# A DLRM tower on one core: products four samples wide in three banks, and a drain with moves on POOL

## The chip, the cores and the metric

One core of a Trainium2 chip runs the whole program. The metric is the device time of one execution in microseconds. The time before is the median of 3 runs.

## What is computed

The reference gathers 26 embedding rows of 64 numbers for each of 2048 samples and a dense vector of 256, and sends them through an interaction block and three layers:

```python
x = layer_norm(dense_t @ Wd.T, gd, bd)
y = layer_norm(jnp.einsum('bnd,ed->bne', sparse_t, Ws), gs, bs)
y = jnp.einsum('bne,pn->bep', y, Wsi)
y = layer_norm(y, gsi, bsi)
y = jnp.swapaxes(y, 1, 2)
T = jnp.concatenate([x[:, None, :], y], axis=1)
Z = jnp.einsum('bnd,bmd->bnm', T, T)
Zflat = Z[:, TRIL_I, TRIL_J]
out = layer_norm(Zflat @ Wl.T, gl, bl) * mask
h = jnp.concatenate([z, r_dense_t], axis=1)
h = jnp.maximum(h @ W_top1 + b_top1, 0.0)
h = jnp.maximum(h @ W_top2 + b_top2, 0.0)
y = h @ W_top3
```

All of it is fp32.

## The kernel before

The batch is cut into 16 units of 128 samples and each unit into four chunks of 32 samples. Each engine has its own program, and every one of them walks the same list of 75 steps. A step does a different stage for chunks of different age: a chunk is transposed (turn, L382) and its Gram products taken (gram, L391) one step after its number, mixed (mix, L405) and projected (project, L416) two steps after, and multiplied with itself (products, L430) four steps after. Work by unit follows: the products are moved to other partitions by DMA (MOVE_AT, 7), multiplied with the weights (flat, L442, in three pieces), normalised and turned back (turn_z, L450). Work by pairs of units (256 samples) is the top layers (top1, L465, in three pieces; top2, L526; top3, L533) and the dense branch (L544, L551, L556). Semaphores alone tie the engines together, and within one engine the order of the step's code holds.

POOL gathers the embedding rows, 26 indirect DMAs for a unit (L314), into three buffers. Before a chunk's gathers it waits until the chunk two before is transposed (turned).

The products of one chunk: tt holds, for WIDE samples at a time, their 34 columns (x, a one, 32 vectors) interleaved. One matmul takes all 32 vectors of WIDE samples as weights and all 34 columns of the same samples as the moving side. Its result holds every pair of the WIDE samples; only pairs of a sample with itself are used. With WIDE at 2 the result has 64 partitions, and two matmuls (q = 0, 1) fill one bank's 128 partitions. A chunk's eight groups of four samples are done in two rounds, one to bank_z and one to bank_t:

```python
WIDE = 2
TILE = PR * WIDE
ROUNDS = ((0, 4), (4, 8))
```

On ACT products_out (L675) copies each round's bank to zbig, with zc_ok counting NR copies a chunk. These banks are shared: bank_z lends its last 32 columns to scale_t (L976), bank_t takes the transposes of turn, bank_u takes the results of mix. squares (L662) come behind products_out on ACT, xcol (L688) and place_sum_x (L697) behind those.

After the last chunk's turn, the drain begins (steps beyond TAIL = 63). There the last two units' flat, turn_z and gains_z have places of their own, tables at flat_of, turn_z_of and gains_z_of. The moves of the last unit are shared out: SP issues those of sample classes j = 0, 1, and ACT, in move_rest (L774), those of j = 2, 3, six of each. relu1 (L736) rectifies the first layer's two pairs of column blocks, gains_z (L727) scales the rows of a turned unit, z_rows (L682) copies the moved products. open_last (L475) starts the last half batch's first layer from the dense part, last1 (L490) finishes it.

Of the kernel before, what the change touches and what calls it, by code (L numbers as in the profile page):

```python
# [44 lines left out]
NU = B // UNIT  # L45
# [16 lines left out]
GROUPS = ((0, 4), (4, 7), (7, 10), (10, 13))  # L62
PIECES = ((0, 2), (2, 4), (4, 6))
HALVES = ((0, 2), (2, 4)), ((4, 6), (6, 7)), ((7, 9), (9, 10)), ((10, 12), (12, 13))
WIDE = 2
TILE = PR * WIDE
ROUNDS = ((0, 4), (4, 8))
NR = len(ROUNDS)


# [93 lines left out]

def gains_z_of(s):
    if s > TAIL + 2:
        return {TAIL + 6: NU - 2, TAIL + 8: NU - 1}.get(s)
    return unit(s, GAINZ_AT)


def half_of(s, steps):
    return steps.index(s) if s in steps else None


def dlrm(nc, x_in, out):
    with ExitStack() as ctx:
# [6 lines left out]
        def sem(name):  # L183
            return ctx.enter_context(nc.semaphore(name))
# [81 lines left out]
        y_ok, sq_ok, ssum_ok, sstd_ok, srs_ok, t_ok = (  # L266
            sem("y_ok"), sem("sq_ok"), sem("ssum_ok"), sem("sstd_ok"), sem("srs_ok"), sem("t_ok"))
        xcol_ok, z_done, zc_ok, sumcol_ok = sem("xcol_ok"), sem("z_done"), sem("zc_ok"), sem("sumcol_ok")
        zs_in, zr_ok = [sem("zs_in0"), sem("zs_in1")], sem("zr_ok")
        flat_done, hst_ok, hmv_ok, hstd_ok, hrs_ok, zn_ok = (  # L270
            sem("flat_done"), sem("hst_ok"), sem("hmv_ok"), sem("hstd_ok"), sem("hrs_ok"), sem("zn_ok"))
        znt_done, zt_ok = sem("znt_done"), sem("zt_ok")
# [27 lines left out]
        @block.gpsimd  # L300
        def _(pool):
            pool.wait_ge(ids_ok, 1)
            for u in range(NU):
                e = u % EB
                for c in range(4):
                    after(pool, mixed, 4 * (u - EB) + min(c + 2, 4))
                    after(pool, turned, 4 * u + c - 1)
                    for part, (t0, t1) in enumerate(HALVES[c]):
                        if part == 1:
                            after(pool, z_done, NR * (4 * u + c - 5) + 1)  # L310
                        for t in range(t0, t1):
                            for a in range(2):
                                col = 2 * TILES * u + 2 * t + a
                                pool.indirect_dma_start(  # L314
                                    emb[:, e, t, D * a:D * a + D], None, x_in["tables"],
                                    bass.IndirectOffsetOnAxis(ap=ids[:, col:col + 1], axis=0),
                                ).then_inc(emb_in[e][c], 16)

        @block.sync
        def _(sp):  # L320
# [47 lines left out]
        def _(pe):  # L368
# [26 lines left out]
            def mix(u, h):  # L395
                e = u % EB
                pieces = mix_pieces(h)
                if u == 0 and h == 0:
                    pe.wait_ge(pre_v, 9)
                pe.wait_ge(scaled, 4 * u + h + 1)  # L400
                after(pe, u_ok, 4 * u + h)
                for c, (t, lo, cnt) in enumerate(pieces):
                    o = PR * (lo - GRP * h)
                    w0 = PR * (lo - first_sample(t))
                    mm = pe.matmul(  # L405
                        bank_u[:, o:o + PR * cnt], emb[:, e, t, :],
                        mix_w[:, t, :, :].rearrange("p s v -> p (s v)")[:, w0:w0 + PR * cnt],
                        start=(c == 0), stop=(c == len(pieces) - 1), skip_group_check=True)
                mm.then_inc(mixed, 1)
# [9 lines left out]
            def products(u, h, i):  # L419
# [1 line left out]
                    pe.wait_ge(t_ok, 4 * u + h + 1)  # L421
                    pe.wait_ge(xcol_ok, u + 1)
                after(pe, zc_ok, NR * (4 * u + h))
                o_bank = (bank_z, bank_t)[i]
                g0, g1 = ROUNDS[i]
                for g in range(g0, g1):
                    for q in range(4 // WIDE):
# [146 lines left out]
            for s in range(STEPS):  # L574
# [11 lines left out]
                    project(*c)  # L586
                pd = chunk(s, PROD_AT)
                if pd:
                    products(*pd, 0)
                    products(*pd, 1)  # L590
                for piece in range(3):
                    j = top1_of(s, piece)
                    if j is not None:
# [5 lines left out]
                j = top2_of(s)  # L599
                if j is not None:  # L600
                    top2(j)
                if s == TAIL + 6:
                    open_last()
                i = x_of(s, 0)
                if i is not None:
                    dense_x(i)
# [9 lines left out]
                j = top3_of(s)  # L616
                if j is not None:
                    top3(j)
                a = half_of(s, LAST1_AT)
                if a is not None:  # L620
                    last1(a)
# [9 lines left out]
        def _(act):  # L631
# [38 lines left out]
            def products_out(u, h, i):  # L670
                act.wait_ge(z_done, NR * (4 * u + h) + i + 1)
                if h == 0 and i == 0:
                    after(act, zs_in[u % 2], 12 * 16 * (u // 2))
                g0, g1 = ROUNDS[i]
                act.copy(zbig[:, u % 2, :, C0:CZ, 8 * h + g0:8 * h + g1],  # L675
                         (bank_z, bank_t)[i][:, 0:ZC * WIDE * (g1 - g0)].rearrange("p (g c w) -> p w c g", c=ZC, w=WIDE)
                         ).then_inc(zc_ok, 1)

            def z_rows(u):
                act.wait_ge(zs_in[u % 2], 12 * 16 * (u // 2 + 1))  # L680
                after(act, flat_done, u)
                act.copy(zr[:, :, :].rearrange("p s (j g) -> p s j g", j=4),  # L682
                         zs[:, :, :, :].rearrange("p j s g -> p s j g")).then_inc(zr_ok, 1)
# [81 lines left out]
                act.wait_ge(y_out, LAST + 1)  # L765
                act.dma_start(out[:, SUP * LAST:SUP * LAST + SUP], yrow[:, :]).then_inc(stored, 16)

            def move_rest():
                act.wait_ge(zc_ok, 4 * NR * NU)
                act.wait_ge(sumcol_ok, NU)  # L770
                act.wait_ge(zr_ok, NU - 1)
                for j in range(2, 4):
                    for part in range(3):
                        act.dma_start(rows_to(j, part), rows_from((NU - 1) % 2, j, part)  # L774
                                      ).then_inc(zs_in[(NU - 1) % 2], 16)

            def relu2(j):
                act.wait_ge(top2_done, j + 1)
                after(act, top3_done, j)
# [12 lines left out]
            for s in range(STEPS):  # L792
# [48 lines left out]
                if se:  # L841
                    root_e(*se)
                if pd:
                    products_out(*pd, 0)
                    products_out(*pd, 1)
                if pj:
                    squares(*pj, 0)
                    squares(*pj, 1)
                if pd == (NU - 1, 3):
                    move_rest()  # L850
                u = col_of(s, XCOL_AT)
                if u is not None:
                    xcol(u)
# [291 lines left out]
```

## Time and profile before

| | |
|---|---|
| median of 3 runs | 590.68 us (590.22 to 592.27) |
| profiled execution | 590.11 us |
| its span, first to last instruction | 588.3 us |
| mean granted TensorE clock | 0.983 of full |
| busy: PE, DVE, ACT, POOL | 523.2, 431.7, 339.3, 394.8 us |

The profile gives busy time by engine and the chain of work that ended last, the groups of instructions by line with what ended the idle time before them, and the timeline. PE is the matmul side of TensorE and PEld its weight loads. An fp32 matmul leaves two records, a transpose one. Times in a timeline are from the start of the span; the "us" of a row reaches to the modelled end of its last instruction, so rows of pipelined matmuls overlap by some tenths of a microsecond, and the distance from one row's start to the next one's start is the time that the work takes.

### The profile page before, as it was taken

Reading aid. Unit: us, or ns where it says so; the run is one execution under the profiler, and the core shown is the slowest. Engines: PE = TensorE matmul, PEld = TensorE weight load, DVE = VectorE, ACT = ScalarE, POOL = GpSimd, SP = SyncE. Lnnn points to the kernel's source line nnn. Section 1 sums busy time; section 2 is a strip of 40 time slices with the busy share of each in tenths; the row PEclk is TensorE's granted clock in tenths of the full one; section 3 lists DMA queues with packets and bytes.
Section 4 is the critical chain, followed back from the end, with each engine's and each line's share of the span. In section 5 each row is a group of like instructions: output and inputs, shape, how many; then the busy total and the mean of one; then the engine's idle time right before and its main releaser. Section 6 shows DMA issues by size and latency. Waiting matters only on the chain.

```text
span 588.3 us, 11685 instructions
## 1 busy us (share of the span) xinstructions
PE 523.2 (89%) x4327; PEld 382.3 (65%) x4327; DVE 431.7 (73%) x806; ACT 339.3 (58%) x731; POOL 394.8 (67%) x420
## 2 busy tenths in 40 slices
PE   0557889597999999997999999998999999989888
PEld 0435656474778667776677767766777767856657
DVE  3579998689677977697877967796787977787210
ACT  1235666466657765575766765675657765766223
POOL 5777777777777777777777777777777777750000
PEclk9997999899899999999999999999999999999999
DMA  6911121212111121212121221212121211110100
GB/s 214 372 47 26 28 54 27 53 28 52 29 42 38 39 62 28 52 30 71 28 46 33 45 56 35 45 31 69 29 52 27 52 31 43 38 34 17 27 0 1
DMA packets 28152, 29.89 MB, mean 51 GB/s; under 512 B 9784, under 2 KB 20544, under 8 KB 27712
## 3 DMA queue, kind: packets, MB, share of 16 engines
q0 software_dynamic: 13312, 13.66, 12.2%
q1 hardware_dynamic: 14456, 15.29, 8.2%
q8 instruction: 35, 0.57, 0.4%
q10 hardware_dynamic: 328, 0.20, 0.1%
q14 instruction: 21, 0.17, 0.1%
HBM read 23.01 MB, written 0.01 MB: 39 GB/s over the span
## 4 chain that ended last, share of the span: by engine, by line
POOL 46%; PE 26%; issue 19%; DMA 4%; DVE 3%; ACT 1%; ACTq 1%; POOLq 0%; SPq 0%
POOL emb L314 46%; PE bank_h L442 5%; PE bank_u L405 4%; DMA emb<-in_tables,ids 3%; PE bank_m L465 3%; PE bank_y L416 3%; PE bank_g L391 2%; PE bank_z L430 2%; PE bank_t L382 2%; PE bank_t L430 1%; PE bank_m L526 1%; DVE part L910 1%; ACTq L774 1%; PE bank_g L490 1%; PE bank_m L533 0%
## 5 line engine op out<-in xcount | busy, mean ns | idle before, releaser
L314 POOL DMA_INDIRECT emb<-in_tables,ids x416 | 394.6, 949 | 130.3 <-issue 123.1
L662 ACT ACTIVATE sq<-tt 128x512 f32<-128x512 f32 x128 | 131.1, 1133 | 4.6 <-DVE tt L963 3.4
L932 DVE TENSOR_TENSOR prod<-bank_g,emb 128x512 f32<-128x512 f32 (+1 forms) x64 | 37.6, 588 | 89.0 <-PE bank_g L391 88.5
L442 PE MATMUL bank_h<-wz,zr 128*128 128x512 f32 x192 | 93.2, 610 | 3.1 <-ACT zt L727 2.1
L405 PE MATMUL bank_u<-mix_w,emb 128*128 128x192 f32 (+4 forms) x512 | 86.0, 314 | 9.7 <-DVE emb L951 9.7
L405 PEld LDWEIGHTS bank_u<-mix_w,emb 128*128 128x128 f32 x512 | 80.3, 200 | 10.9 <-DVE emb L951 10.9
L963 DVE TENSOR_TENSOR tt<-bank_y,biasc 128x512 f32<-128x512 f32 x128 | 81.9, 681 | 2.5 <-PE bank_y L416 2.5
L644 ACT COPY embt<-bank_t 128x512 f32<-128x512 f32 (+1 forms) x64 | 32.5, 507 | 82.4 <-PE bank_t L382 82.2
L980 DVE TENSOR_TENSOR tt<-tt,bank_z 128x1024 f32<-128x1024 f32 x64 | 78.1, 1220 | 2.2
L970 DVE TENSOR_REDUCE ssum<-sq 128x32 f32<-128x1024 f32 x64 | 77.5, 1211 | 1.1 <-ACT sq L662 1.0
L416 PE MATMUL bank_y<-us,proj 64*128 64x512 f32 x256 | 73.0, 647 | 0.7 <-ACT us L654 0.7
L430 PEld LDWEIGHTS bank_z<-tt 128*64 128x64 f32 x1024 | 35.4, 137 | 48.5 <-issue 47.4
L391 PE MATMUL bank_g<-gram_w,embt 128*128 128x128 f32 x416 | 61.9, 290 | 1.7 <-ACT embt L644 1.7
L382 PE MATMUL bank_t<-eye,emb 128*128 128x128 f32 x208 | 36.3, 290 | 27.5 <-DMA emb<-in_tables,ids 27.5
L654 ACT COPY us<-bank_u 128x512 f32<-128x512 f32 x64 | 37.5, 586 | 40.2 <-PE bank_u L405 40.1
L391 PEld LDWEIGHTS bank_g<-gram_w,embt 128*128 128x128 f32 x416 | 55.2, 202 | 2.7 <-ACT embt L644 2.5
L382 PEld LDWEIGHTS bank_t<-eye,emb 128*128 128x128 f32 x208 | 25.1, 146 | 48.5 <-DMA emb<-in_tables,ids 37.5
L442 PEld LDWEIGHTS bank_h<-wz,zr 128*128 128x128 f32 x192 | 33.8, 190 | 30.7 <-issue 26.8
L649 ACT ACTIVATE std<-var 128x8 f32<-128x8 f32 (+1 forms) x64 | 13.6, 212 | 56.4 <-DVE var L942 54.1
L430 PE MATMUL bank_z<-tt 128*64 128x68 f32 x1024 | 44.5, 229 | 0.0
L430 PE MATMUL bank_t<-tt 128*64 128x68 f32 x1024 | 41.2, 223 | 0.0
L465 PE MATMUL bank_m<-zt,w 128*128 128x256 f32 x168 | 40.8, 379 | 0.0
(121 smaller groups left out, 622.5 us busy)
## 6 DMA issues: line engine op xcount, KB each, us to landing
emb<-in_tables,ids POOLq DMA_INDIRECT x416, 2.4
zs<-zbig SPq DMA_DIRECT2D x62, 40.5 KB
zs<-zbig SPq DMA_DIRECT2D x62, 36.0 KB
dense<-in_dense SPq DMA_DIRECT2D x8, 256.0 KB, 5.1
wfull<-in_wfull SPq DMA_DIRECT2D x1, 2048.0 KB, 10.2
wz<-in_wrows SPq DMA_DIRECT2D x1, 1536.0 KB, 13.2
w<-in_w SPq DMA_DIRECT2D x1, 1280.0 KB, 13.9
zs<-zbig SPq DMA_DIRECT2D x62, 16.5 KB
```

What stands on the lines that cost most here:

```text
L314: pool.indirect_dma_start(emb[:, e, t, D * a:D * a + D], None, x_in["tables"], bass.IndirectOffsetOnAxis(ap=ids[:, col:col + 1], axis=0),) ...
L382: mm = pe.transpose(bank_t[:, P * (t - t0):P * (t - t0) + P], emb[:, e, t, :], eye[:, :])
L391: mm = pe.matmul(bank_g[:, o:o + P], embt[:, k % 2, o:o + P], gram_w[:, :], start=True, stop=True)
L405: mm = pe.matmul(bank_u[:, o:o + PR * cnt], emb[:, e, t, :], mix_w[:, t, :, :].rearrange("p s v -> p (s v)")[:, w0:w0 + PR * cnt], start=( ...
L416: mm = pe.matmul(bank_y[a][:, :], proj[q, :], us[q, h % 2, :], start=True, stop=True)
L430: mm = pe.matmul(o_bank[TILE * q:TILE * q + TILE, o:o + ZC * WIDE], some[:, C0 * WIDE:ZC * WIDE], some, start=True, stop=True)
L442: mm = pe.matmul(bank_h[:, :], zr[:, s, :], wz[:, s, :], start=(s == 0), stop=(s == SLOTS - 1))
L465: mm = pe.matmul(bank_m[:, SUP * (c % 2):SUP * (c % 2) + SUP], w1[:, t, P * c:P * c + P], rhs, start=(t == 3), stop=(t == 2))
L662: A(sq[:, GRP * a:GRP * a + GRP, :].rearrange("p (q w) v -> p q v w", w=WIDE), tt[:, u % 2, q0:q0 + n, C0:ZC, :], ACT.Square).then_inc(sq_ ...
L963: TT(tt[:, u % 2, q0:q0 + n, C0:ZC, :], bank_y[a][:, :].rearrange("p (q w v) -> p q v w", w=WIDE, v=PR), biasc[:, :].unsqueeze(1).unsqueez ...
L970: dve.tensor_reduce(ssum[:, h % 2, :], sq[:, :, :], AX.X, ALU.add).then_inc(ssum_ok, 1)
L980: TT(y, y, srs.rearrange("p (q w) -> p q w", w=WIDE).unsqueeze(2).broadcast_to([P, n, PR, WIDE]), ALU.mult).then_inc(t_ok, 1)
```

## The change

WIDE becomes 4: one matmul takes four samples, 128 weight columns and 136 moving columns, and fills all 128 partitions (so the loop over q has one turn). Three such results fit in a bank, so the eight groups go in three rounds of 3, 3 and 2, to bank_z, bank_t and bank_u. Mix, which writes bank_u, gets a wait for the copies of the chunk products that used it. tt, zbig and rows_from follow WIDE. In the drain the six moves of move_rest go from ACT's queue to POOL's, behind its last gather, with a semaphore of their own (zs_rest); gains_z of unit 14 moves from step TAIL + 6 to TAIL + 5, where it stands between the two rectified pairs; open_last moves from behind top2 in step TAIL + 6 to behind top3 in step TAIL + 7.

```diff
-WIDE = 2
+WIDE = 4
 TILE = PR * WIDE
-ROUNDS = ((0, 4), (4, 8))
+ROUNDS = ((0, 3), (3, 6), (6, 8))
...
     if s > TAIL + 2:
-        return {TAIL + 6: NU - 2, TAIL + 8: NU - 1}.get(s)
+        return {TAIL + 5: NU - 2, TAIL + 8: NU - 1}.get(s)
...
+            pool.wait_ge(zc_ok, 4 * NR * NU)
+            pool.wait_ge(sumcol_ok, NU)
+            pool.wait_ge(zr_ok, NU - 1)
+            for j in range(2, 4):
+                for part in range(3):
+                    pool.dma_start(rows_to(j, part), rows_from((NU - 1) % 2, j, part)
+                                  ).then_inc(zs_rest, 16)
...
                 after(pe, u_ok, 4 * u + h)
+                after(pe, zc_ok, NR * (4 * u + h - 2))
...
-                o_bank = (bank_z, bank_t)[i]
+                o_bank = (bank_z, bank_t, bank_u)[i]
...
-                    products(*pd, 0)
-                    products(*pd, 1)
+                    for i in range(NR):
+                        products(*pd, i)
...
-                if s == TAIL + 6:
-                    open_last()
                 i = x_of(s, 0)
...
                     top3(j)
+                if s == TAIL + 7:
+                    open_last()
...
             def z_rows(u):
-                act.wait_ge(zs_in[u % 2], 12 * 16 * (u // 2 + 1))
+                if u < NU - 1:
+                    act.wait_ge(zs_in[u % 2], 12 * 16 * (u // 2 + 1))
+                else:
+                    act.wait_ge(zs_in[u % 2], 12 * 16 * (u // 2) + 6 * 16)
+                    act.wait_ge(zs_rest, 6 * 16)
...
-                    products_out(*pd, 0)
-                    products_out(*pd, 1)
+                    for i in range(NR):
+                        products_out(*pd, i)
...
-                if pd == (NU - 1, 3):
-                    move_rest()
```

On the PE, in a step of the steady part, from gram to the next step's transposes. Before:

```order
L391 MATMUL bank_g<-gram_w,embt 128x128 x3
L416 MATMUL bank_y<-us,proj 128x512 x2
L430 MATMUL bank_z<-tt 64x68 x8
L430 MATMUL bank_t<-tt 64x68 x8
L442 MATMUL bank_h<-wz,zr 128x512 x2
```

After (the lines are numbered anew, L438 is products):

```order
L398 MATMUL bank_g<-gram_w,embt 128x128 x3
L424 MATMUL bank_y<-us,proj 128x512 x2
L438 MATMUL bank_z<-tt 128x136 x3
L438 MATMUL bank_t<-tt 128x136 x3
L438 MATMUL bank_u<-tt 128x136 x2
L450 MATMUL bank_h<-wz,zr 128x512 x2
```

Sixteen matmuls with 64 result partitions and 68 columns have become eight with 128 and 136.

On ACT, in the drain, from the last unit's products to the scaling of unit 14 (L736 rectifies, L727 scales, L682 is z_rows). Before:

```order
L675 COPY zbig<-bank_t 128x2x34x4
L774 DMA zs<-zbig 22x1x192
L774 DMA zs<-zbig 48x1x192
L774 DMA zs<-zbig 54x1x192
L774 DMA zs<-zbig 22x1x192
L774 DMA zs<-zbig 48x1x192
L774 DMA zs<-zbig 54x1x192
L736 ACTIVATE h<-bank_m,vecs 128x256 x2
L682 COPY zr<-zs 128x768
L736 ACTIVATE h<-bank_m,vecs 128x256 x2
L727 ACTIVATE zt<-bank_h,vecs 128x128 x3
```

After:

```order
L683 COPY zbig<-bank_t 128x4x34x3
L683 COPY zbig<-bank_u 128x4x34x2
L748 ACTIVATE h<-bank_m,vecs 128x256 x2
L739 ACTIVATE zt<-bank_h,vecs 128x128 x3
L694 COPY zr<-zs 128x768
L748 ACTIVATE h<-bank_m,vecs 128x256 x2
L784 ACTIVATE h<-bank_m,vecs 128x256 x2
```

The six moves are gone from ACT's queue, the scaling stands ahead of z_rows and the second pair, and z_rows waits for POOL's moves too.

On the PE, at the end of the drain, from flat of unit 15 on. Before:

```order
L442 MATMUL bank_h<-wz,zr 128x512 x6
L526 MATMUL bank_m<-h,w 128x256 x8
L475 MATMUL bank_t<-dense,w 128x128 x2
L475 MATMUL bank_u<-dense,w 128x128 x2
L475 MATMUL bank_y<-dense,w 128x128 x4
L450 MATMUL bank_h<-eye,zn 128x128 x3
L533 MATMUL bank_m<-h,vecs 1x256 x2
L490 MATMUL bank_g<-dense,w 128x128 x2
```

After:

```order
L450 MATMUL bank_h<-wz,zr 128x512 x6
L534 MATMUL bank_m<-h,w 128x256 x8
L458 MATMUL bank_h<-eye,zn 128x128 x3
L541 MATMUL bank_m<-h,vecs 1x256 x2
L483 MATMUL bank_t<-dense,w 128x128 x2
L483 MATMUL bank_u<-dense,w 128x128 x2
L483 MATMUL bank_y<-dense,w 128x128 x4
L498 MATMUL bank_g<-dense,w 128x128 x2
```

The eight matmuls of open_last have gone from before turn_z to behind top3.

## Rows read from the trace of the kernel before

**Rows 1.** The page: busy times by engine, and the chain by line.

```profile
PE 523.2 (89%) x4327; PEld 382.3 (65%) x4327; DVE 431.7 (73%) x806; ACT 339.3 (58%) x731; POOL 394.8 (67%) x420
...
POOL emb L314 46%; PE bank_h L442 5%; PE bank_u L405 4%; DMA emb<-in_tables,ids 3%; PE bank_m L465 3%; PE bank_y L416 3%; PE bank_g L391 2%; PE bank_z L430 2%; PE bank_t L382 2%; PE bank_t L430 1%; PE bank_m L526 1%; DVE part L910 1%; ACTq L774 1%; PE bank_g L490 1%; PE bank_m L533 0%
```

**Rows 2.** Groups: busy us, mean ns | idle before; waits: us in total, times, longest.

```profile
L314 POOL DMA_INDIRECT emb<-in_tables,ids x416 | 394.6, 949 | 130.3 <-issue 123.1 <-DVE ids L871 3.9 <-PE bank_t L382 3.0
...
POOL emb L314 <- issue: 123.1, 404, 0.3
```

**Rows 3.** Stretches of 65 us from 170 to 495 us, their sum and mean.

```profile
sum 325.00, PE 315.13 PEld 230.85 DVE 258.06 ACT 209.61 POOL 245.76; mean PE 63.03 PEld 46.17 DVE 51.61 ACT 41.92 POOL 49.15
```

**Rows 4.** Waits of PE, 148 to 528 and 60 to 148 us; timeline at 147.

```profile
PE bank_t L382 <- DMA emb<-in_tables,ids: 11.6, 10, 2.5
...
PE bank_t L382 <- DMA emb<-in_tables,ids: 12.2, 5, 4.9
...
147.36 1.07 PE L382 MATMUL bank_t<-eye,emb 128*128 128x128 f32 x4 [4.16 <-DMA emb<-in_tables,ids]
```

**Rows 5.** Timeline of PE in one step: start us, us, what.

```profile
304.92 1.13 PE L416 MATMUL bank_y<-us,proj 64*128 64x512 f32 x4
305.98 0.69 PE L430 MATMUL bank_z<-tt 128*64 128x68 f32 x16
306.50 0.64 PE L430 MATMUL bank_t<-tt 128*64 128x68 f32 x16
307.07 1.13 PE L465 MATMUL bank_m<-dense,w 128*128 128x256 f32 x4
```

**Rows 6.** Groups by form: the gram matmuls.

```profile
L391 PE MATMUL bank_g<-gram_w,embt 128*128 128x128 f32 x416 | 61.9, 290 | 1.7 <-ACT embt L644 1.7
```

**Rows 7.** The chain in the drain: start us, us, what.

```profile
524.42 2.49 DMA emb<-in_tables,ids
...
561.78 5.39 PE bank_h L442 x12
...
574.15 4.66 PE bank_g L490 x40
```

**Rows 8.** Timeline of ACT in a short step.

```profile
196.00 0.33 ACT L688 COPY tt<-xs 128x128 f32<-128x128 f32 x1
196.22 0.47 ACT L644 COPY embt<-bank_t 128x384 f32<-128x384 f32 x1
```

**Rows 9.** Groups by form on ACT.

```profile
L662 ACT ACTIVATE sq<-tt 128x512 f32<-128x512 f32 x128 | 131.1, 1133 | 4.6 <-DVE tt L963 3.4
...
L675 ACT COPY zbig<-bank_z 128x272 f32<-128x272 f32 x64 | 24.7, 386 | 5.2 <-PE bank_z L430 3.1 <-ACT yrow L788 0.3
L644 ACT COPY embt<-bank_t 128x384 f32<-128x384 f32 x48 | 23.1, 481 | 35.2 <-PE bank_t L382 35.0
```

**Rows 10.** Timeline of ACT in the drain (ACTq issues the moves).

```profile
549.00 5.14 ACTq L774 DMA_DIRECT2D zs<-zbig  x6
554.24 0.84 ACT L736 ACTIVATE h<-bank_m,vecs 128x256 f32<-128x256 f32 x2 [5.27 <-issue]
555.73 0.83 ACT L682 COPY zr<-zs 128x768 f32<-128x768 f32 x1 [0.65 <-DMA zs<-zbig]
559.75 0.84 ACT L736 ACTIVATE h<-bank_m,vecs 128x256 f32<-128x256 f32 x2 [3.19 <-PE bank_m L465]
```

**Rows 11.** Timeline of PE in the drain.

```profile
552.57 0.49 PE L450 MATMUL bank_h<-eye,zn 128*128 128x128 f32 x3
555.13 1.13 PE L465 MATMUL bank_m<-dense,w 128*128 128x256 f32 x4 [2.07 <-ACT h L736]
...
570.46 0.61 PE L475 MATMUL bank_t<-dense,w 128*128 128x128 f32 x4
...
571.35 1.06 PE L475 MATMUL bank_y<-dense,w 128*128 128x128 f32 x8
572.65 0.55 PE L450 MATMUL bank_h<-eye,zn 128*128 128x128 f32 x3 [0.24 <-DVE zn L1014]
```

More of the change, by code:

```diff
@@ L268, in dlrm @@
         xcol_ok, z_done, zc_ok, sumcol_ok = sem("xcol_ok"), sem("z_done"), sem("zc_ok"), sem("sumcol_ok")
-        zs_in, zr_ok = [sem("zs_in0"), sem("zs_in1")], sem("zr_ok")
+        zs_in, zs_rest, zr_ok = [sem("zs_in0"), sem("zs_in1")], sem("zs_rest"), sem("zr_ok")
         flat_done, hst_ok, hmv_ok, hstd_ok, hrs_ok, zn_ok = (
@@ L675, in products_out @@
                 act.copy(zbig[:, u % 2, :, C0:CZ, 8 * h + g0:8 * h + g1],
-                         (bank_z, bank_t)[i][:, 0:ZC * WIDE * (g1 - g0)].rearrange("p (g c w) -> p w c g", c=ZC, w=WIDE)
+                         (bank_z, bank_t, bank_u)[i][:, 0:ZC * WIDE * (g1 - g0)].rearrange("p (g c w) -> p w c g", c=ZC, w=WIDE)
                          ).then_inc(zc_ok, 1)
             def z_rows(u):
-                act.wait_ge(zs_in[u % 2], 12 * 16 * (u // 2 + 1))
+                if u < NU - 1:
[3 more added lines that the diff above has]
+                    act.wait_ge(zs_rest, 6 * 16)
                 after(act, flat_done, u)
@@ L766, in last_store @@
                 act.dma_start(out[:, SUP * LAST:SUP * LAST + SUP], yrow[:, :]).then_inc(stored, 16)
[L768 to L775, printed above, removed]
             def relu2(j):
```

## The prediction, made before the run

> **What bounds the kernel now.** I read the page's busy times and its chain first, then the groups of POOL, then the stretches, then the waits of the PE, and last the timeline of one step. The page shows the PE busy 89% of the span and a chain in which the gathers of line L314 hold 46% [rows 1]. POOL issues 416 gathers of 949 ns and sits 0.30 us before each (123.1 us over 404) [rows 2], so a unit of 26 gathers takes 26 x 1.25 = 32.5 us, and the 16 units fill 519 us. That is the pace. The PE is close behind it: over five stretches of 65 us (two units each) it is busy 315.1 us of 325 at a granted clock of 1.00, the 2.4 GHz level [rows 3]. From 148 to 528 us its only idle time is ten waits for gathered rows, 11.6 us together; from 60 to 148 us there are 12.2 us more [rows 4]. So the PE has 11.6 us to give away over the last 47 steps, 0.25 us a step. Anything above that, per step, becomes the new pace.
>
> **Part 1, products four samples wide.** In a step the two rounds of products stand between project (L416, at 304.92) and the next work: they start at 305.98, and the next line starts at 307.07 [rows 5]. That is 1.09 us for 32 records (each fp32 matmul leaves two records: 16 matmuls, and x16 in each of two rows), 34 ns a record of 68 columns. One column at full array width costs 5.39 us / (12 x 512) = 0.877 ns for wide records, and 4.66 / (40 x 128) = 0.91 ns for narrow ones, both back to back in the drain [rows 7]. At 0.877 a record of 68 columns would take 60 ns. The 34 ns can only be two records running side by side, one in each half of the array's columns (q = 0 and q = 1 write partitions 0 to 63 and 64 to 127).
>
> The change has 8 matmuls of 128x136 in a step, 16 records, and each fills the array, so nothing runs beside it: 16 x 136 x 0.877 = 1.91 us. The step grows by 1.91 - 1.09 = 0.82 us. The useful work is the same; the wide form computes 4x4 blocks of sample pairs, of which 4 of 16 are kept, where the narrow one kept 2 of 4. Ends of this price: if the wide record ran like project's, which pays (305.98 - 304.92) / (4 x 512) = 0.52 ns a column [rows 5], the block would take 1.13 us and the step would grow by 0.04; if it ran at the mean of the gram matmuls, 149 ns for 128 columns (61.9 us over 416 records) [rows 6], it would take 2.53 us and the growth would be 1.44. The first needs half an array; the second mean has waits for the ACT in it. I take 0.82 and hold 0.7 to 1.0 as likely.
>
> Of the 1.09 us now, 16 pairs x 60 ns explain 0.95, so 0.14 us at most is the cost of entering and leaving the half-width form. If it is paid after the change too, the growth is 0.96, and the result 47 x 0.14 = 6.6 us later. The Trainium skill (TensorEngine Tiling, section Key Properties) says that a change of tiling mode, not of tile alone, drains the engine. By that rule one mode fewer in each step saves this time, which is the 0.82; no run here shows it apart.
>
> From the wait that ends at 147 us to the last transpose (chunk 63, at 527) there are 47 steps. The wait before them, 4.16 us [rows 4], is longer than the 4 x 0.82 us gained since the last one, so the lag starts near zero there; earlier steps cost nothing because they lie in the 12.2 us of waits. The lag at chunk 63 is 47 x 0.82 - 11.6 = **26.9 us**. POOL is then held by the PE (it waits for turned), but it has two PE steps, some 17 us, for at most 8 x 1.25 + 2.49 = 12.5 us of gathers and landing [rows 2, 7], so no new wait comes from it. With no gather waits left, all of the PE's time is work.
>
> **Part 2, three banks and three copies.** The ACT copies now take 272 elements in 386 ns; from 384 in 481 ns [rows 9] the slope is 0.85 ns. 408, 408 and 272 elements make 500 + 500 + 386 = 1.39 us against 0.77: 0.62 us more a step. The third bank's copy can start only after the products' end, so by my estimate it ends near P + 2.5 us (P = start of products; 1.91, some 0.2 to start, 0.39), against P + 1.6 now (1.09 in place of 1.91). Squares (1133 ns each, overlapping a little) and in some steps one more copy (0.33 us) follow, and only then the next embt copy: in one short step it starts at 196.22, the moment its predecessor in the queue is through [rows 8]. The PE comes to it 0.8 us later than now and the ACT 0.9 us later, so about nothing is lost in most steps, and a few tenths in the two short steps of every eight: 12 x 0.17, call it **2 us**. Unknown is how runs of three elements are written instead of four. Lower end: no cost. Upper end: the rate of the scattered writes of the squares, 1133 ns for 512 [rows 9], 2.2 ns each. Three copies then take 2.4 us. That is a rival below. The new wait before mix (bank_u free) asks for what the transposes before it have waited for already; it costs 0. The DVE waits for the same copies before it scales with bank_z; its queue is busy 51.6 us of 65 in two units [rows 3], so 0.
>
> **Part 3, the drain.** Three blocks of products (chunks 60 to 62) put 2.5 us before the last one, and its own copies end 0.9 us later in the block and a little more: the moves start some 3.1 us later than 549.00 (relative to the lag). Now ACT issues six moves in 5.14 us, and the first rectified pair sits behind them until 554.24 [rows 10], though its products were done before the PE's turn_z at 552.57 [rows 11]. After the change POOL issues them, so the pair runs at 552.6 + 3.3 = 555.9, 1.7 us later than now. The PE's third piece starts 0.9 us after the pair and takes 4.6 us (555.13 to 559.75 now [rows 10, 11]), so it ends at 555.9 + 0.9 + 4.6 = 561.4. The row scaling of unit 14 (1.16 us) goes in beside it. The moved rows: six on POOL from 552.1. Lower bound for one is ACT's 0.84 us with 1.6 us to landing (554.14 to 555.73), upper is a gather's 1.25 us with its 2.49 [rows 2, 7]: landing at 558.7 to 562.1, copied 0.83 us later, 559.5 to 562.9. I take the middle, under the PE's 561.4. So flat of unit 15 starts between 561.4 and 562.9, against 561.78 now [rows 7]: **0**, up to +1.1. Nothing else is queued behind POOL's wait: it has no gathers left.
>
> open_last goes the other way. Now its 16 records (570.46 to 572.4) fill the gap in which the DVE normalises, and turn_z waits only 0.24 us more [rows 11]. After the change they stand behind turn_z and top3; the gap stays (relu2 and the root are still before the normalising), and 16 x 0.117 = **1.9 us** come onto the path.
>
> **Sum.** 26.9 + 2 + 0 + 1.9 = 30.8 us. The profiled execution took 590.11 us (588.3 of span and 1.8 around it): 590.1 + 30.8 = **620.9 us**. That execution lies 0.6 us under the median of the runs, 590.68, so 621 is about 30.5 us over the median, 5.1%.
>
> **The rivals.**
> - The copies become the loop (0.12). If runs of three and two are written at the squares' rate, the last copy ends near P + 3.5, the squares near P + 5.6, and the next embt copy and the gram behind it come 0.9 us late in two short steps of eight. In favour: the squares' 1133 ns. Against: runs of four cost nothing over contiguous writes [rows 9]. 12 x 0.9 us = 11 more in place of my 2, with a little in other steps: 632 us.
> - The wide products are nearly free (0.07), the case that ends on the other side. It decides at 0.25 us a step, that is 1.34 us for the block or 84 ns a record. Only project's half-array rate (70 ns) is under that. Steady state stays at POOL's 32.5 us; in the drain the pair starts 1.5 us earlier, flat 1.7 to 3.6 us earlier, open_last takes back 1.9: 588.4 to 590.3, say 589.4 us. Against it: 117 ns back to back for full-width records of 128 columns [rows 7].
> - A fixed cost in every matmul, now paid half as often (0.05). If 25 ns of each of the 34 ns were fixed and not shared, the 16 records saved would give back 0.4 us: growth 0.42, lag 47 x 0.42 - 11.6 = 8.1, with 2 + 1.9: 602 us. Against it: 128 and 512 columns cost nearly the same per column [rows 7]. The Trainium skill (TensorEngine Tiling, section Instruction Overhead) gives such a fixed cost of about 60 cycles a matmul; the trace, with 34 ns a record for 68 columns, leaves no room for it.
> - Something I have not seen, such as DVE and ACT waiting in turn (0.06): 635 us and more.
>
> **How the numbers follow.** My forecast has 0.70. Its own range: growth 0.7 to 1.0 gives lags of 21.3 to 35.4, the rest 1 to 6: 612 to 631. With the copies' case the range is 607 to 635, which leaves out under 2 in 10. About 0.3% is what a measurement of this kernel can tell from no change. Faster needs the nearly free case and a quick POOL: 0.03; within 0.3% is the rest of it: 0.04; slower: 0.93.
>
> **What would show it.** Right: POOL waits for bank_t transposes in nearly every chunk; the PE's gather waits vanish after 150 us; product blocks of about 1.9 us, 117 to 125 ns from record to record; units of 34.8 us or a little over; the six POOL moves done by 559 plus the lag; 1.9 us of open_last behind top3. Wrong: units still at 32.5 us (the block is under 1.34 us), or embt and us copies that the PE waits for in most steps (the ACT's loop), or POOL moves of well over 1.25 us each.

## The result and the profile after

The changed kernel takes 615.45 us (median of 4 runs, 615.4 to 615.79), against 591.42 us for the kernel before in the same session: a ratio of 1.042 (95% interval 1.0403 to 1.044), so slower. (The ratios of this document are not quotients of the two medians beside them; here the medians give 1.0406.) The profiled execution took 615.44 us with a span of 613.3 us, 25.0 us more than the 588.3 before. The forecast was 621.0, with a range of 607 to 635.

The page of the changed kernel, busy times and the chain by engine and by line:

```profile
PE 567.7 (93%) x3303; PEld 433.7 (71%) x3303; DVE 439.5 (72%) x806; ACT 371.3 (61%) x779; POOL 398.0 (65%) x426
...
PE 81%; POOL 8%; DVE 4%; issue 3%; DMA 2%; ACT 2%; SPq 0%; ACTq 0%; POOLq 0%
PE bank_h L450 13%; PE bank_m L473 10%; PE bank_u L413 10%; PE bank_y L424 9%; PE bank_z L438 8%; POOL emb L314 8%; PE bank_g L398 7%; PE bank_t L438 6%; PE bank_u L438 4%; PE bank_m L534 4%; PE bank_t L389 4%; DMA emb<-in_tables,ids 2%; PE bank_m L541 1%; PE bank_m L552 1%; DVE part L911 1%
```

The gathers held 46% of the chain [rows 1] and hold 8% now. The PE is busy 44.5 us more with 1024 records fewer. Its waits (us in total, times, longest) from 148 to 555 us, and below them those of POOL over the span:

```profile
PE bank_t L389 <- DMA emb<-in_tables,ids: 2.2, 1, 2.2
...
POOL emb L314 <- issue: 119.4, 391, 0.6
POOL emb L314 <- PE bank_t L389: 22.3, 19, 2.0
```

The one wait of the PE for rows is at 147.82 and stands against the 4.16 us before [rows 4]; the ten after it are gone, and now POOL waits for the PE, 19 times. That is once or twice a unit; the forecast had it in nearly every chunk. Five stretches of 70 us, a little over two units each, from 170 to 520 us, their sum and mean:

```profile
sum 350.00, PE 349.95 PEld 268.85 DVE 267.35 ACT 233.63 POOL 253.52; mean PE 69.99 PEld 53.77 DVE 53.47 ACT 46.73 POOL 50.70
```

The PE has 0.05 us left in 350, where it had 9.9 in 325 [rows 3]. Four chunks, from one unit's first transposes to the next one's, now take 34.2 us (183.59 to 525.94 is ten units), where 34.8 was forecast; before, the same ten took 32.4 each (181.56 to 505.62, in both kernels chunks 20 to 60). The PE's timeline of one step, which answers to [rows 5]:

```profile
303.71 1.13 PE L424 MATMUL bank_y<-us,proj 64*128 64x512 f32 x4
304.77 0.96 PE L438 MATMUL bank_z<-tt 128*128 128x136 f32 x6
305.57 0.86 PE L438 MATMUL bank_t<-tt 128*128 128x136 f32 x6
306.27 0.63 PE L438 MATMUL bank_u<-tt 128*128 128x136 f32 x4
306.73 1.03 PE L473 MATMUL bank_m<-dense,w 128*128 128x256 f32 x4
307.59 1.46 PE L473 MATMUL bank_m<-zt,w 128*128 128x256 f32 x6
```

The block of products takes 306.73 - 304.77 = 1.96 us, 122 ns a record, in place of 1.09 us. But the first four records behind it take 307.59 - 306.73 = 0.86 us, and took 308.04 - 307.07 [rows 5] = 0.97 us; the row that followed before:

```profile
308.04 1.46 PE L465 MATMUL bank_m<-zt,w 128*128 128x256 f32 x6
```

The step is therefore longer by 0.76 us. The turns of the two kernels, compared chunk by chunk, fall apart by 0.75 to 0.77 us in most steps in which the kernel before had no wait, and by about 0.70 in the step behind a long one.

The copies of ACT by form (busy us, mean ns | idle before them), for [rows 9]:

```profile
L683 ACT COPY zbig<-bank_t 128x408 f32<-128x408 f32 x64 | 41.0, 640 | 9.0 <-PE bank_t L438 8.9
L683 ACT COPY zbig<-bank_z 128x408 f32<-128x408 f32 x64 | 32.2, 504 | 15.1 <-PE bank_z L438 14.5 <-ACT yrow L791 0.3
L683 ACT COPY zbig<-bank_u 128x272 f32<-128x272 f32 x64 | 26.0, 407 | 0.0
```

The PE in the drain, which answers to [rows 7, 11], and POOL's and ACT's part of it, which answer to [rows 10]:

```profile
569.42 0.86 PE L438 MATMUL bank_z<-tt 128*128 128x136 f32 x6
...
576.68 1.13 PE L473 MATMUL bank_m<-dense,w 128*128 128x256 f32 x4 [0.60 <-ACT h L748]
...
579.80 1.46 PE L473 MATMUL bank_m<-zt,w 128*128 128x256 f32 x6
583.29 7.11 PE L450 MATMUL bank_h<-wz,zr 128*128 128x512 f32 x12 [2.02 <-ACT zr L694]
590.24 3.62 PE L534 MATMUL bank_m<-h,w 128*128 128x256 f32 x16
595.88 0.55 PE L458 MATMUL bank_h<-eye,zn 128*128 128x128 f32 x3 [2.02 <-DVE zn L1015]
596.36 1.02 PE L541 MATMUL bank_m<-h,vecs 128*1 128x256 f32 x4
597.31 0.71 PE L483 MATMUL bank_t<-dense,w 128*128 128x128 f32 x4
597.86 0.61 PE L483 MATMUL bank_u<-dense,w 128*128 128x128 f32 x4
598.30 1.06 PE L483 MATMUL bank_y<-dense,w 128*128 128x128 f32 x8
599.20 0.61 PE L498 MATMUL bank_g<-dense,w 128*128 128x128 f32 x4
```

```profile
572.32 3.39 POOL L323 DMA_DIRECT2D zs<-zbig  x6 [30.34 <-ACT zbig L683]
```

```profile
575.79 0.84 ACT L748 ACTIVATE h<-bank_m,vecs 128x256 f32<-128x256 f32 x2 [3.76 <-PE bank_m L473]
581.36 1.16 ACT L739 ACTIVATE zt<-bank_h,vecs 128x128 f32<-128x128 f32 x3 [4.74 <-PE bank_m L473]
582.40 0.83 ACT L694 COPY zr<-zs 128x768 f32<-128x768 f32 x1
```

The scaling of unit 14 stands behind the third piece, z_rows behind the scaling, and flat waits 2.02 us for both. Where the 25.0 us come from:

| place | lag over before, us | since the line above |
|---|---|---|
| turn of chunk 63 (526.96, now 547.20) | 20.2 | |
| flat of unit 15 (561.78, now 583.29) | 21.5 | +1.3 |
| top2 (567.01, now 590.24) | 23.2 | +1.7 |
| turn_z (572.65, now 595.88) | 23.2 | 0 |
| last1 | 25.1 | +1.9 |
| end of span | 25.0 | -0.1 |

Three groups of runs follow. The last group, and of the second group the run with one change of half, were on two other chips, on which the kernel before takes 763.65 and 773.73 us (medians of 35 and 29). The executions read there are interrupted by pauses, of 2 to 3 us in the place read most closely (the narrow kernel with its moves on POOL, 400 to 406 us: POOL idle 2.19 us, DVE 2.93, ACT 3.26, the PE going on in pieces). Of these runs only the ratios and undisturbed stretches of the timeline are read. The ratios compare, of each kernel, only its executions within 1.5% of its fastest, and the medians are of all, so the two can point different ways.

### The profile page after: what moved, and what is told of

It reads as the page before. It is cut to its first block, busy times and chain, and to the rows that moved or that the text cites. A ratio compares the mean times of both kernels' runs of the same rounds, so it can differ in the third digit from the quotient of the medians.

```text
span 613.3 us, 9685 instructions
## 1 busy us (share of the span) xinstructions
PE 567.7 (93%) x3303; PEld 433.7 (71%) x3303; DVE 439.5 (72%) x806; ACT 371.3 (61%) x779; POOL 398.0 (65%) x426
## 3 DMA queue, kind: packets, MB, share of 16 engines
q0 software_dynamic: 13504, 13.85, 11.6%
## 4 chain that ended last, share of the span: by engine, by line
PE 81%; POOL 8%; DVE 4%; issue 3%; DMA 2%; ACT 2%; SPq 0%; ACTq 0%; POOLq 0%
PE bank_h L450 13%; PE bank_m L473 10%; PE bank_u L413 10%; PE bank_y L424 9%; PE bank_z L438 8%; POOL emb L314 8%; PE bank_g L398 7%; PE bank_t L438 6%; PE bank_u L438 4%; PE bank_m L534 4%; PE bank_t L389 4%; DMA emb<-in_tables,ids 2%; PE bank_m L541 1%; PE bank_m L552 1%; DVE part L911 1%
## 5 line engine op out<-in xcount | busy, mean ns | idle before, releaser
L450 PE MATMUL bank_h<-wz,zr 128*128 128x512 f32 x192 | 91.5, 603 | 2.0 <-ACT zr L694 2.0
L413 PE MATMUL bank_u<-mix_w,emb 128*128 128x192 f32 (+4 forms) x512 | 84.0, 309 | 9.0 <-DVE emb L952 9.0
L413 PEld LDWEIGHTS bank_u<-mix_w,emb 128*128 128x128 f32 x512 | 78.5, 196 | 9.7 <-DVE emb L952 9.7
L438 PEld LDWEIGHTS bank_z<-tt 128*128 128x128 f32 x384 | 48.8, 190 | 48.2 <-issue 47.3
L438 PE MATMUL bank_z<-tt 128*128 128x136 f32 x384 | 61.5, 297 | 0.0
L438 PE MATMUL bank_t<-tt 128*128 128x136 f32 x384 | 55.0, 279 | 0.0
L438 PEld LDWEIGHTS bank_t<-tt 128*128 128x128 f32 x384 | 49.3, 190 | 0.0
L683 ACT COPY zbig<-bank_t 128x408 f32<-128x408 f32 x64 | 41.0, 640 | 9.0 <-PE bank_t L438 8.9
```

The costliest lines, as they stand in the source:

```text
L413: mm = pe.matmul(bank_u[:, o:o + PR * cnt], emb[:, e, t, :], mix_w[:, t, :, :].rearrange("p s v -> p (s v)")[:, w0:w0 + PR * cnt], start=( ...
L438: mm = pe.matmul(o_bank[TILE * q:TILE * q + TILE, o:o + ZC * WIDE], some[:, C0 * WIDE:ZC * WIDE], some, start=True, stop=True)
L450: mm = pe.matmul(bank_h[:, :], zr[:, s, :], wz[:, s, :], start=(s == 0), stop=(s == SLOTS - 1))
```

## The experiments

**Theory.** The steady part costs some 20 us since wide products lose the overlap of two half-width matmuls; the drain's edits cost the rest. **Rivals.** The copies or the third round cost it, not the products; or the drain's edits do.

### The wide products alone, and the drain alone

The first is the changed kernel with move_rest on ACT, gains_z and open_last as before. The second is the kernel before with the three drain edits of the change:

```diff
-        return {TAIL + 6: NU - 2, TAIL + 8: NU - 1}.get(s)
+        return {TAIL + 5: NU - 2, TAIL + 8: NU - 1}.get(s)
...
-                if s == TAIL + 6:
-                    open_last()
+                if s == TAIL + 7:
+                    open_last()
...
-                    move_rest()
```

(move_rest goes to POOL as in the change.)

> The wide products in three banks alone, with the drain as it was before (moves on ACT, scaling of unit 14 in step TAIL + 6, open_last behind top2). Theory: the whole loss of the steady part is the PE's block of products, so the last transposes stand at 547.2 us as in the changed kernel (20.2 us late) and POOL waits for bank_t. In the drain: last copies end at 572.0, ACT issues until 577.2, the first pair at 577.3, third piece to 582.8, second pair, scaling, flat of unit 15 at about 584.9 (changed kernel: 583.3), but open_last lies in its gap again, 1.9 us back, and if flat runs at the full clock as before, 1.7 us more: 613.2 us in all, 2 us under the changed kernel. Rival: the drain edits bring what they were put in for, so without them it takes 617 us or more.

> The three drain edits alone, with products two samples wide. Theory: the PE's steady part is that of the kernel before, last transposes at 527.0. The first pair runs at 552.8 in place of 554.2, the third piece ends at 558.2, but the scaling of unit 14 waits for that piece (it overwrites rows that the piece reads), so the scaling takes 558.3 to 559.5, the copy of the moved rows until 560.3, flat of unit 15 starts at 560.3 (1.5 us earlier), open_last costs 1.9: 590.5 us; if flat falls to the low clock as in the changed kernel, 592.2. Rival (my prediction's picture): the scaling runs beside the third piece and flat starts at 558.2 to 559: 588.5 us.

Measured, with the kernel before at 590.37 us (median of 19): wide alone 612.92 us (612.74 to 613.07), ratio 1.037 (1.0343 to 1.0398); the drain alone 592.27 us (590.87 to 593.92, 10 runs), ratio 1.002 (1.0004 to 1.0036). So the products carry 22.5 of the changed kernel's surplus of some 25 us, and the other 2.5 come with the drain's edits (0.4 of them ahead of the drain, where the two kernels do the same work: the last products start at 568.98 and 569.42). The PE of the wide kernel in its drain:

```profile
568.98 0.86 PE L431 MATMUL bank_z<-tt 128*128 128x136 f32 x6
...
584.41 5.39 PE L443 MATMUL bank_h<-wz,zr 128*128 128x512 f32 x12 [2.07 <-ACT zt L728]
```

From the last products to flat it takes 15.43 us, the changed kernel 583.29 - 569.42 = 13.87: the drain's edits do bring flat 1.6 us forward. They lose it again, and 2 us more, in two places, open_last (1.9 us) and flat itself (5.39 became 7.11). The second place is told by the drain alone, PE timeline:

```profile
560.46 7.11 PE L449 MATMUL bank_h<-wz,zr 128*128 128x512 f32 x12 [2.03 <-ACT zr L693]
...
574.49 1.11 PE L482 MATMUL bank_t<-dense,w 128*128 128x128 f32 x4
```

and by the stretches of 2 us in it, first the drain alone, then the changed kernel (us, busy us of the engines, granted clock, DMA share, GB/s):

```profile
562.00:564.00 2.00, 2.00 (x4) 0.86 (x3) 0.00 (x0) 0.00 (x0) 0.00 (x0) 0.50 0.00 0
...
576.00:578.00 2.00, 2.00 (x12) 2.00 (x11) 0.00 (x0) 0.00 (x0) 0.00 (x0) 0.50 0.00 0
```

```profile
584.00:586.00 2.00, 2.00 (x3) 0.69 (x3) 0.00 (x0) 0.00 (x0) 0.00 (x0) 0.53 0.00 0
586.00:588.00 2.00, 2.00 (x4) 0.87 (x3) 0.00 (x0) 0.00 (x0) 0.00 (x0) 0.62 0.00 0
```

Behind the gap ahead of flat the clock was granted at the lower of its two levels, 1.2 GHz, for about 3.4 us (worked out from the shares above, 0.53 and 0.62 of full), and flat pays for it. The drain alone met it twice, in flat and again in open_last, which took 574.49 to 577.95, 3.46 us for 1.89. Its profiled span is 3.8 us over that of before and its median only 1.9 us, so not every execution has both.

### What in the products costs: rounds, copies, or overlap

The narrow kernel, first with three rounds, banks, copies and the wait before mix, as the change has them:

```diff
-ROUNDS = ((0, 4), (4, 8))
+ROUNDS = ((0, 3), (3, 6), (6, 8))
...
+                after(pe, zc_ok, NR * (4 * u + h - 2))
...
-                o_bank = (bank_z, bank_t)[i]
+                o_bank = (bank_z, bank_t, bank_u)[i]
```

> Products two samples wide, but in three rounds (3, 3, 2 groups) to three banks with three copies, and the new wait of mix: what the change does to ACT and the banks, without the wide matmuls. Theory: the PE's block stays 1.1 us and the copies cost about 0.2 us more a step on ACT, which has room: 590 to 592 us. Rival (copies and the bank wait form a loop with the PE): 595 us or more, with waits of PE for zbig or embt copies.

Measured 590.64 us (590.0 to 592.43, 10 runs), ratio 1.0004 (0.9988 to 1.002). The page's waits of the PE:

```profile
PE bank_t L382 <- DMA emb<-in_tables,ids: 27.7, 19, 5.0
```

That is the total of the span, and before it was 27.5 us in 18 waits, of which [rows 4] has the two parts that matter here. So the third round, the third copy and the wait before mix cost nothing. The copies here have half the elements (204, 204 and 136, in 329, 401 and 290 ns), so the length of the wide ones isn't covered by this run, and is read from the changed kernel: no wait of the PE for ACT in its steady part.

Then the narrow kernel with the loop over q outside that over g, so that all matmuls of one half of the columns come before those of the other, in each round. The work is the same:

```diff
-                for g in range(g0, g1):
-                    for q in range(4 // WIDE):
+                for q in range(4 // WIDE):
+                    for g in range(g0, g1):
```

> The kernel before with only the order of its narrow products changed: in each round all four groups of the lower half (q = 0), then all four of the upper half (q = 1), instead of lower and upper by turns. Same matmuls, same number, same data. Theory: 34 ns a record came from two halves running side by side; in turn they take about 60 ns, the block 1.8 to 1.9 us in place of 1.09, and the kernel becomes as slow as the wide one, 609 to 614 us. Rival (a fixed cost in every matmul, or weight loads, set the 34 ns): nothing changes, 590 to 592 us.

Measured 599.09 us (596.06 to 599.54), ratio 1.0118 (1.008 to 1.0156): slower, by 8.7 us where 19 to 24 were expected. Neither had said this. Its PE timeline tells why (start us, us):

```profile
301.24 0.80 PE L430 MATMUL bank_z<-tt 128*64 128x68 f32 x13
301.83 0.27 PE L430 MATMUL bank_t<-tt 128*64 128x68 f32 x1
301.88 0.22 PE L430 MATMUL bank_z<-tt 128*64 128x68 f32 x1
301.94 0.22 PE L430 MATMUL bank_t<-tt 128*64 128x68 f32 x1
...
302.06 0.75 PE L430 MATMUL bank_t<-tt 128*64 128x68 f32 x13
302.74 1.13 PE L465 MATMUL bank_m<-dense,w 128*128 128x256 f32 x4
```

Records of bank_z and bank_t alternate in time although the code has all of bank_z first: the upper half of bank_z runs beside the lower half of bank_t. The block takes 1.50 us. The same timeline accounts for the time of the whole:

```profile
533.35 0.49 PE L382 MATMUL bank_t<-eye,emb 128*128 128x128 f32 x3
...
569.49 7.08 PE L442 MATMUL bank_h<-wz,zr 128*128 128x512 f32 x12 [2.07 <-ACT zt L727]
```

The transposes of chunk 63 are 533.35 - 526.96 = 6.4 us late, the three blocks behind them add 1.2, and flat took 7.08 in place of 5.39: 9.3 us of the 9.4 between the two spans (597.7 and 588.3). The block has three changes of half, and several matmuls overlap at each. So I made one with a single change, by ordering lower bank_z, lower bank_t, upper bank_z, upper bank_t:

```diff
-                for g in range(g0, g1):
-                    for q in range(4 // WIDE):
+                halves = ((0, 0), (0, 1), (1, 0)) if i == 0 else ((1, 1),)
+                for q, r in halves:
+                    o_bank = (bank_z, bank_t)[r]
+                    g0, g1 = ROUNDS[r]
+                    for g in range(g0, g1):
```

> As halves in turn, but the lower halves of both banks first and then the upper halves of both, so that there is one place in a step where lower gives way to upper, in place of three. In the trace of the run with three such places the block took 1.50 us, 0.41 under the 1.91 that 32 x 60 ns make, 0.14 for each place where the two halves overlap. Theory: with one place the block takes about 1.77 us, the step grows by 0.68, and 47 steps less the 15.5 us of slack that the two traces show make 16.5 us more at the last transposes: 606 to 611 us. Rival (something else in the reordering cost the 9 us): as slow as halves in turn, 599 us.

This one ran on the third chip: 784.61 us (781.75 to 788.65), ratio 1.0202 (1.012 to 1.0285). Its time on a chip like the first can't be read from that. Its block can:

```profile
302.99 0.69 PE L431 MATMUL bank_z<-tt 128*64 128x68 f32 x8
303.51 0.46 PE L431 MATMUL bank_t<-tt 128*64 128x68 f32 x5
...
303.99 0.46 PE L431 MATMUL bank_z<-tt 128*64 128x68 f32 x5
304.28 0.64 PE L431 MATMUL bank_t<-tt 128*64 128x68 f32 x8
304.85 0.48 PE L466 MATMUL bank_m<-dense,w 128*128 128x256 f32 x1
```

1.86 us for the same 32 records, 58 ns each, in place of 34; 1.77 was expected. (The five records from 303.99 to 304.28, which nothing overlaps, also take 58 ns each.) The same 16 matmuls take 1.86 us with one change of half, 1.50 with three and 1.09 where every matmul changes it; the wide form takes 1.96. That shows what the 0.82 us of the forecast rested on: the narrow form's advantage is the running side by side of its two halves.

### The drain

On the second chip, the changed kernel with open_last back where it was (behind top2), and the kernel before with the moves on POOL and nothing else. The edit of the first:

```diff
+                if s == TAIL + 6:
+                    open_last()
...
-                if s == TAIL + 7:
-                    open_last()
```

> The changed kernel with open_last back behind top2 (step TAIL + 6); all else as changed. Theory: open_last's 16 records fill the 2 us in which the DVE normalises the last unit, so 1.9 us come back: 613.6 us. Rival: the gap is filled by something else or the matmuls then delay turn_z: within 0.3 us of the changed kernel, 615.4.

> The kernel before with only the six last moves issued by POOL. Theory: the first pair starts when its products are done, 552.8 in place of 554.2, so the third piece, second pair and scaling, and with them flat of unit 15, come 1.4 us earlier, at 560.3: 588.7 us against 590.1 of the kernel before. Rival: POOL's moves land so late (after 560) that z_rows takes over as the end: no change.

Then both with the scaling of unit 14 freed of the third piece. The last half batch gets its own buffer for turned rows, so nothing that the piece reads is overwritten, and the scaling runs between the rectified pairs. In the narrow one (the wide one has the same edit; both have open_last behind top2):

```diff
-        return {TAIL + 6: NU - 2, TAIL + 8: NU - 1}.get(s)
+        return {TAIL + 5: NU - 2, TAIL + 8: NU - 1}.get(s)
...
+        zt_last = sb("zt_last", [P, 3, SUP])
...
-                if u % 2 == 0:
+                to = zt if u < NU - 2 else zt_last
+                if u % 2 == 0 and u < NU - 2:
```

> The kernel before with the moves on POOL and the scaling of unit 14 between the two pairs, and with a buffer of its own for the last two units' scaled rows, so that this scaling need not wait for the third piece of top1; open_last stays behind top2. Theory: scaling runs at 553.7 to 554.8 beside the third piece, the moved rows are copied by 556.5, and flat of unit 15 starts right behind the third piece at 558.2, 3.6 us earlier than before: 586.5 us. Rival: the copies of moved rows or stats come late and take the place of the scaling: 588 us or more.

> The changed kernel with that buffer and with open_last back. Theory: relative to the changed kernel, flat starts at 581.3 in place of 583.3 with no idle time of 2 us before it, so it also keeps the high clock (5.3 us in place of 7.0), and open_last gives back 1.9: 2.0 + 1.7 + 1.9 = 5.6 us, 609.8 us. If the low clock in flat does not hang on that idle time: 611.5 us.

These three were repeated on the third chip, for the ratios:

> The same kernel as e5, on another chip. Theory: 588.7 us, 1.4 us under the kernel before, from the first pair's earlier start. The run of all three drain edits showed POOL's six moves issued in under 4 us and early enough. Rival: no change.

> The same kernel as e7, on another chip. Theory: flat of unit 15 starts behind the third piece with no idle time, at 558.2 in place of 561.8: 586.5 us, 3.6 us under the kernel before. If the scaling is not what flat waits for, no more than e5b gives.

> The same kernel as e8, on another chip: the changed kernel with a buffer of its own for the last two units' rows and open_last back behind top2. Theory: 2.0 us of idle before flat, 1.7 us of low clock in flat and 1.9 us of open_last come back: 609.8 us against the changed kernel's 615.4 and 612.9 of the wide products alone. If the low clock stays: 611.5.

| kernel | median of all, us | ratio (95%) | last products to end of span, us |
|---|---|---|---|
| before (first chip) | | | 41.24 |
| changed (first) | | | 43.88 |
| wide alone (first) | | | 41.92 |
| changed, open_last back | 766.54 | 1.0001 (0.9952 to 1.0051) | 40.45 |
| narrow, moves on POOL | 762.29 | 0.9987 (0.9945 to 1.0029) | 39.81 |
| the same, third chip | 768.08 | 1.0002 (0.995 to 1.0055) | 39.73 |
| narrow, own rows | 758.9 | 0.9917 (0.9872 to 0.9962) | 37.48 |
| the same, third chip | 767.14 | 0.9922 (0.987 to 0.9974) | 37.49 |
| wide, own rows | 766.25 | 0.9946 (0.9892 to 1.0) | 38.16 |
| the same, third chip | 766.69 | 0.9973 (0.9926 to 1.002) | 38.13 |

The stretch from the last products on has no pause in the executions shown, and its records are as long as on the first chip (5.39 us for twelve, 3.62 for sixteen), so it can be compared. With open_last back the changed drain is 3.4 us shorter. 1.9 of that is open_last; 1.7 is that flat ran at the upper clock level there, behind a gap of the same 2.03 us (last1's first records take back 0.1). POOL's moves alone bring 1.4 to 1.5 us. The times that were expected are those of the first chip and can't be tested on these two; the expected gains can, by this last column: 1.4 for POOL's moves, 3.6 for the narrow kernel with own rows (3.76 came), 5.6 for the wide one (5.7 came), and 1.9 for open_last, where 3.4 came with the clock.

With the buffer the order of the wide kernel's drain becomes, on ACT and then on the PE:

```profile
736.87 1.16 ACT L741 ACTIVATE zt_last<-bank_h,vecs 128x128 f32<-128x128 f32 x3
738.77 0.83 ACT L695 COPY zr<-zs 128x768 f32<-128x768 f32 x1 [0.74 <-DMA zs<-zbig]
```

```profile
741.45 5.31 PE L451 MATMUL bank_h<-wz,zr 128*128 128x512 f32 x12
746.60 3.62 PE L535 MATMUL bank_m<-h,w 128*128 128x256 f32 x16
```

The scaling is through before the rows land, flat follows the third piece with no idle time and runs in 5.31 us. The scaling's wait for the third piece was worth 2.3 us: 40.45 less 38.16 in the wide kernel with open_last back, from which this one differs by the buffer alone, and 39.81 less 37.48 from the narrow one with its moves on POOL, where the scaling's place changes with the buffer. Altogether the drain is 5.75 us shorter than the changed kernel's (open_last and the clock in flat are the rest), and 3.8 us shorter in the narrow form than that of before.

On these two chips the ratio says little of the products: the wide kernel with open_last back stands level with the kernel before (1.0001), with a drain only 0.8 us shorter. Its PE is busy 80% of the span there and waits for other engines, 58.9 us for embt copies alone; that its 0.76 us a step is therefore not paid in full is argued and not shown. Why those chips pause was not tried.

The narrow kernel with own rows is the one version whose interval lies under 1 on both chips, at 0.8%. Its drain accounts for 0.5% (3.76 us of 764), which both intervals hold. On a chip like the first its drain alone, 3.76 us of 590.4, would give some 586.6 us (an estimate; it did not run there).

## Why the prediction was right, and where it was not

The direction, the mechanism and the range held: 615.4 us for 621.0, in the case that had 0.70. The sum was 30.8 us over before and came out at 25.0 by terms that erred both ways: 8.7 us too much in the steady part and its copies, 3.0 too little in the drain. That the total is nearer than its parts is luck.

- **Part 1, growth of a step: 0.82 us, measured 0.76.** The block itself came out a little longer than costed (1.96 for 1.91). What was left out is the 0.10 us that the work behind it gains. The prediction had considered a cost of leaving the half-width form of up to 0.14 us, but looked for it inside the block; part of it lay in the next line's first records. Over 47 steps this is 3 us. Another place shows the same 0.1: behind top3, whose results have one partition, the first four records of open_last take 597.86 - 597.31 = 0.55 us, and the next four, alike, 0.44. The Trainium skill (TensorEngine Tiling, section Key Properties) says that a change of tiling mode drains the engine; the 0.10 us a step saved with one mode less agrees with it.
- **Part 1, slack: 11.6 us, measured 15.3.** The lag at chunk 63 was 20.2 us, and 47 x 0.755 = 35.5 us had been added, so 15.3 us were soaked up. This term was off most, by 3.7 us. Two things were missing. A wait as the profile shows it begins at the modelled end of the row before, which reaches past the real one. The lag shows the real wait: at chunk 32 (278.18, now 283.92) it fell from 7.56 to 5.74 us while a step's 0.76 came on, so 2.6 us were soaked up where the row shows 2.36. The ten waits, 0.16 to 0.30 us each, make 2.2 us. And before, the steps behind the 4.16 us wait ran at the lower clock level (the row at 147.36 took 1.07 us for four records [rows 4], the same row takes 0.66 now): the lag was 0.46 us at chunk 16 and -0.30 at chunk 17, so 1.5 us came back there.
- **Part 2, copies: 2 us, measured none.** Their cost was about as bounded, 504, 640 and 407 ns for the 500, 500 and 386, 1.55 us for 1.39. But the PE shows no wait for embt or us in its steady part. It comes to those lines later by the growth, and the ACT has kept up. The rival of the copies as the loop needed 2.2 ns an element; 640 / 408 = 1.6 is the worst that was met. No rows show what makes the bank_t copy 136 ns longer than bank_z's of the same form.
- **Part 3, flat: 0, up to +1.1, measured +1.3.** The step "the row scaling of unit 14 goes in beside it" was wrong. gains_z of an even unit waits for top1_done: it overwrites the rows that the third piece still reads. The piece itself was in time: its last row starts at 579.80 and takes 1.3 us, which is 560.9 without the 20.2 us of lag, where 561.4 was forecast. Only then came 1.16 of scaling, a z_rows that had been moved behind it in the queue, and flat. The kernels with a buffer of their own show it.
- **Part 3, POOL's moves: 0.84 to 1.25 us each, measured 0.57** (3.39 for six). This lies under both bounds: the bound from below, ACT's own price (which [rows 10] gives as 5.14 / 6 = 0.86 and not 0.84), was no bound for another engine. The rows were there early; they waited for ACT.
- **Part 3, open_last: 1.9, measured 1.89.** The gap it used to fill stayed open, 2.02 us at 595.88.
- **Not foreseen: the clock in flat, 1.7 us.**

In numbers: 20.2 in place of 26.9, 0 for 2, 1.3 for 0, 1.7 for nothing, 1.9 for 1.9: 25.1.

Of the rivals, nearly free wide products and a fixed cost a matmul are out: the block took 1.96 us where they needed 1.34 and 1.5. The Trainium skill's fixed cost of about 60 cycles (TensorEngine Tiling, section Instruction Overhead) does not appear here either, taken as an addition to every matmul: records of half the columns that don't overlap take half the time, 58 ns for 68 columns against 122 for 136. The same section also says that one column takes as long as 60, and no run here has a matmul that short.

## What to carry to other kernels

Before matmuls are made wider to have fewer of them, look whether the narrow ones run side by side: time by the distance from record to record, against columns times the price of a full-width one. When a wait on one engine is costed as slack for another, read it from the lag between steps, since shown waits are too short by the modelled end before them. And when an instruction is moved up in a queue, list what it waits for and what it overwrites, as a semaphore may hold it, and all behind it, where it was.

## What the hardware showed that was not expected

- Half-width matmuls overlap only where neighbours in the queue use different halves, and then over the bounds of banks: 34 ns a record of 68 columns alternating, 58 ns with one change of half in 32 records.
- A gap of 2.0 to 2.1 us on the PE before flat was followed by some 3.4 us at the 1.2 GHz level in the profiles of four kernels (the changed one, the drain alone, halves in turn with a flat of 7.08 us, and one change of half with 7.09), and by none in six profiles of five others (before [rows 7], wide alone, narrow in three rounds, open_last back, and the narrow kernel with POOL's moves on both chips). The four profiles without the gap did not show it. What decides it stays open, and it need not be the kernel, as all but the repeats have one profile each: of the 19 executions of the kernel before, twelve took 589.7 to 590.7 us at a mean clock of 0.980 to 0.983, and seven 591.8 to 592.8 at 0.974 to 0.977. So the 1.7 us in flat may belong to an execution and not to the change, though all four executions of the changed kernel lie within 0.4 us.
- The six moves of the narrow kernel were issued in 3.40 us by POOL, 0.57 each, and in 5.14 by ACT [rows 10], 0.86 each.
